# Mixture of experts in a five-layer block: rows gathered by expert through DRAM in 78 blocks of 128 rows, instead of all rows through each expert in use

## The reference, cut to what matters

```python
scores = sigmoid(xf @ gate_w + bias)
top_scores, top_idx = top_k(scores, 2)
top_scores = top_scores / (sum(top_scores) + 1e-06)
w = zeros((T, E)).at[arange(T)[:, None], top_idx].add(top_scores)
hact = gelu(einsum('th,ehi->tei', xf, up_w) + up_b)
eo = einsum('tei,eih->teh', hact, down_w) + down_b
combined = einsum('teh,te->th', eo * 0.1, w)
shared = (gelu(xf @ sw_up + sb_up) @ sw_down + sb_down) * 0.1
out = (shared + combined); out = out / (max(abs(out)) + 1e-06)
x = x + 0.5 * out
```

## Time and profile before

| | |
|---|---|
| median of 3 runs | 1553.57 us (1551.65 to 1554.36) |
| the profiled execution's own time | 1552.47 us |
| its span, first to last instruction | 1550.7 us |
| PE busy in the span | 1394.1 us (90%) |
| DVE, ACT, POOL busy | 61%, 52%, 26% |
| mean granted PE clock | 0.946 of full |
| m1 / m2 in the span | 664.1 to 965.5 / 1258.9 to the end |

### The profile page before, as it was taken

The page is one execution under the profiler, slowest core; times in us unless marked ns, Lnnn a source line. Parts: engine busy times, 40 slices in busy tenths (PEclk is TensorE's granted clock), DMA queues, the critical chain, the costliest instruction groups (busy, mean ns, idle before and its releaser), DMA issues. The chain is left out here.

```text
span 1550.7 us, 22874 instructions
## 1 busy us (share of the span) xinstructions
PE 1394.1 (90%) x7314; PEld 729.1 (47%) x7314; DVE 947.5 (61%) x1896; ACT 801.6 (52%) x1465; POOL 400.0 (26%) x585
## 2 busy tenths in 40 slices
PE   2896899999999879799999997899998779999997
PEld 1672222222222257567777764122221157777776
DVE  5677688889889347451222256699899941222236
ACT  0220688888888714354343354665666444443432
POOL 4021232322330012220000002788888710000000
PEclk9996799999999979889999998799999979999999
DMA  4020121222211010000000000444444300000001
GB/s 94 0 83 1 62 73 52 63 72 72 79 66 43 1 19 1 1 16 1 17 16 1 17 1 23 159 157 140 146 133 154 111 1 16 16 15 2 16 14 42
DMA packets 81206, 77.31 MB, mean 50 GB/s; under 512 B 21004, under 2 KB 60376, under 8 KB 81112
## 3 DMA queue, kind: packets, MB, share of 16 engines
q1 hardware_dynamic: 78992, 75.85, 15.7%
q10 hardware_dynamic: 2120, 0.28, 0.2%
HBM read 55.78 MB, written 16.78 MB: 47 GB/s over the span
## 5 line engine op out<-in xcount | busy, mean ns | idle before, releaser
L1375 ACT ACTIVATE m_hidden<-m_pU,m_up_b 128x512 f32<-128x512 f32 x320 | 219.8, 687 | 265.6 <-PE m_pU L1524 265.4
L1183 DVE TENSOR_REDUCE at_nm<-at_mx 128x2 f32<-128x1024 f32 x256 | 303.8, 1219 | 40.4 <-PE at_mx L1026 39.0
L1531 PEld LDWEIGHTS m_pD<-m_down,m_hidden 128*128 128x128 f32 x2560 | 296.7, 192 | 32.5 <-issue 32.5
L1531 PE MATMUL m_pD<-m_down,m_hidden 128*128 128x128 f32 x2560 | 297.1, 275 | 0.0
L1129 ACT ACTIVATE at_probs<-at_ring 128x512 f32<-128x512 f32 x512 | 269.2, 605 | 47.3 <-PE at_ring L1038 45.8
L1524 PE MATMUL m_pU<-m_xT_all,m_up 128*128 128x512 f32 x640 | 291.2, 601 | 1.1 <-PEq L305 0.5
L1500 DVE TENSOR_TENSOR m_out_b<-m_pD,m_down_b 128x512 f32<-128x512 f32 x64 | 44.2, 691 | 288.6 <-PE m_pD L1531 288.6
L1524 PEld LDWEIGHTS m_pU<-m_xT_all,m_up 128*128 128x128 f32 x640 | 118.0, 193 | 123.7 <-issue 123.5
L2023 POOL TENSOR_TENSOR ss_hc<-ss_h,ss_c_all 128x512 f32<-128x512 f32 x128 | 161.9, 1271 | 52.1 <-DVE ss_h L2195 44.6
L1038 PE MATMUL at_ring<-at_qq,at_kk 51*128 51x512 bf16 x512 | 163.3, 386 | 7.1 <-ACT at_probs L1129 6.1
L1026 PE MATMUL at_mx<-at_kk,at_qq 48*128 48x512 bf16 x512 | 156.0, 398 | 12.7 <-DVE at_nm L1183 8.1
(11 more groups left out here) (282 smaller groups left out, 1511.1 us busy)
## 6 DMA issues: line engine op xcount, KB each, us to landing
ss_dtb<-ss_dt_rows SPq DMA_DIRECT2D x128, 256.0 KB
at_qq<-q_stack SPq DMA_DIRECT2D x64, 96.0 KB, 2.3
at_kk<-k_stack SPq DMA_DIRECT2D x64, 96.0 KB, 2.3
q_stack<-at_qs SPq DMA_DIRECT2D x8, 384.0 KB, 2.6
k_stack<-at_ks SPq DMA_DIRECT2D x8, 384.0 KB, 3.0
ss_stack<-ss_parts SPq DMA_DIRECT2D x96, 32.0 KB, 2.7
X<-in_L_attn_x_dram SPq DMA_DIRECT2D x8, 256.0 KB, 6.1
q_stack<-at_qs SPq DMA_DIRECT2D x8, 256.0 KB, 2.9
```

What stands on the lines that cost most here:

```text
L1183: dve.tensor_reduce(nm[group % 2][:, 2 * (pair % 2) + parity, 2 * half:2 * half + 2], mx[parity][:, :, :], AX.X, ALU.max, negate=True).the ...
L1375: act.activation(hidden[t % 2][:, k, :], pU[k][:, :], ACT.Gelu, bias=up_b[buf][:, k:k + 1]).then_inc(s.gelu_done, 1)
L1531: last = pe.matmul(pD[t % 2][:, c, :], hidden[t % 2][:, k, c * P:(c + 1) * P], down[buf][:, k, :], start=(k == 0), stop=(k == NI - 1))
```

## The change

The dense passes of the listed experts are replaced by blocks of gathered rows; the shared expert's pass and the router stay.

- **Routing.** `hot[0]` and `hot[1]` stay apart, and `weight[k]` is each row's weight for its first and second expert. Two products on PE at t = 1 of the shared pass give each row's rank among the rows of its expert (`v.below`) and the totals. 16 links on DVE turn them into the row's place in a DRAM buffer, `index`, and into the expert of each block, `expert_of`. The chain of dependent steps has 37 links instead of 31.
- **Scatter.** The rows are cut into two halves of four sequences (`HALVES`). POOL scatters the rows of a tile of 128, with identity and weight behind them (130 floats, 520 bytes), to `sorted_rows` by an indirect transfer: 16 tiles for each half and choice, 64 transfers in all. Between the first and the second choice of a half it waits for the landing, since the same tile is marked anew.
- **Blocks.** Each expert's rows start on a multiple of 128 in the half's buffer, which has 39 blocks of 128 rows; all 2 x 39 = 78 are worked off whether they are full or not (8192 row-expert pairs fill 64). For block j SP loads the rows (`load_block`, ring of 8) and the expert's up weights (`load_up`, 256 KB, ring of 6); PE turns the rows (`turn`), ACT copies them, PE makes four up products with 128 columns, ACT four gelus of 128 x 128, PE four down products, DVE adds the bias and multiplies by the weight (ring `y` of 12), and POOL scatters the block to `pair_rows` (`put`), a second indirect transfer. All engines that need it read the block's expert by a register load. All experts' down weights stay in SBUF.
- **Return.** `pair_rows` is loaded for each sequence and choice (`load_results`) and added to `acc`, which now lies over `xT_all`. The first four sequences are finished in between the blocks of the second half, in five pieces each; the last four after the last block.
- **Scan's lead.** The same steps as before, spread over blocks of m1's second half (`LEAD_AT`, `LEAD_POOL_AT`, `SILU_AT`).
- **Elsewhere.** Both DRAM buffers are filled with an empty row from SP early in f1 (two transfers of 78 x 128 rows of 520 bytes), ahead of the first `write_stacks`; attention waits at its end for the fill. f2 and the scan write the normalised rows to a buffer for all rows (`v.rows`) and so wait for no transposition. A pair of barriers with a clearing of semaphores comes after m1. Biases of all experts are loaded in f2.

```diff
+HALVES = 2
+HS, HT = NB // HALVES, NT // HALVES
+HB = (2 * HT * P + E1 * (P - 1)) // P
+TB = HALVES * HB
+X_BUFS, Y_BUFS, T_BUFS, U_BUFS = 8, 12, 3, 6
+FINISH_AT, PIECES = 8, 5
+Y_LOAD_AT = {11: (0, 1), 18: (2,), 23: (3,)}
+LEAD_AT = {14: 3, 19: 4, 22: 5, 25: 6, 28: 7, 36: 8, 38: 9}
...
+def fill_sorted(sp, r):
+    sp.wait_ge(r.made, 2)
+    for rows in r.sorted:
+        sp.dma_start(rows.rearrange("(j p) d -> p j d", p=P), r.empty[:, :].unsqueeze(1).broadcast_to([P, TB, ROW])
+                     ).then_inc(r.filled, 16)
...
+            def load_block(j):
+                if j >= X_BUFS:
+                    sp.wait_ge(s.y_ready, j - X_BUFS + 1)
+                sp.dma_start(xb[:, j % X_BUFS, :], sorted_rows[j * P:(j + 1) * P, :]).then_inc(xb_in[j % X_BUFS], 16)
+            def load_up(j):
+                e = expert_at(sp, j)
+                if j >= U_BUFS:
+                    sp.wait_ge(s.bup_done, j - U_BUFS + 1)
+                sp.dma_start(up_now[j % U_BUFS][:, :], ins["L1_ffn_up_w"][e]).then_inc(up_in[j % U_BUFS], 16)
...
+            for half in range(HALVES):
+                for k in range(2):
+                    sp.wait_ge(scattered[half][k], 16 * HT)
+                for j in range(HB):
+                    load_block(half * HB + j)
+                    load_up(half * HB + j)
...
+            wait_written(TB)
+            for b in range(HS, NB):
+                load_results(b)
...
+            def scatter(half, k, t):
+                at_tile = half * HT + t
+                pool.indirect_dma_start(sorted_rows, bass.IndirectOffsetOnAxis(ap=index[:, k, at_tile:at_tile + 1], axis=0),
+                                        v.rows[:, at_tile, :], None, bounds_check=TB * P - 1, oob_is_err=False
+                                        ).then_inc(scattered[half][k], 16)
+            def put(j):
+                pool.wait_ge(s.y_ready, j + 1)
+                pool.indirect_dma_start(pair_rows, bass.IndirectOffsetOnAxis(ap=y_id[j % Y_BUFS][:, :], axis=0),
+                                        y[j % Y_BUFS][:, :], None, bounds_check=PAIR_ROWS - 1, oob_is_err=False
+                                        ).then_inc(y_out[j % Y_BUFS], 16)
...
+            pool.wait_ge(s.placed, 1)
+            for t in range(HT):
+                scatter(0, 0, t)
+            pool.wait_ge(scattered[0][0], 16 * HT)
+            mark(0, 1)
+            for t in range(HT):
+                scatter(0, 1, t)
+            mark(1, 0)
+            for t in range(HT):
+                scatter(1, 0, t)
+            pool.wait_ge(scattered[1][0], 16 * HT)
+            mark(1, 1)
+            for j in range(HB):
+                if j < HT:
+                    scatter(1, 1, j)
+                put(j)
...
+            for j in range(TB):
+                after = expert_at(act, j + 1) if j + 1 < TB else None
+                gelus(j, e)
+                if j + 2 < TB:
+                    take_turned(j + 2)
+                if lead is not None and j - HB in LEAD_AT:
+                    scan_lead_act(act, g, q=ahead, s=lead, t=LEAD_AT[j - HB])
...
+                if j >= Y_BUFS:
+                    dve.wait_ge(y_out[j % Y_BUFS], 16 * (j // Y_BUFS))
+                dve.wait_ge(xb_in[j % X_BUFS], 16 * (j // X_BUFS + 1))
+                dve.tensor_copy(y_id[j % Y_BUFS][:, :], xb[:, j % X_BUFS, ID:ID + 1])
+                dve.wait_ge(s.bdown_done, j + 1)
+                dve.tensor_tensor(yt[j % 2][:, :], pD[j % 2][:, 0, :],
+                                  v.down_b[:, bass.ds(e, 1), :].rearrange("p a d -> p (a d)"), ALU.add
+                                  ).then_inc(s.y_taken, 1)
+                dve.wait_ge(s.y_taken, j + 1)
+                dve.tensor_scalar(y[j % Y_BUFS][:, :], yt[j % 2][:, :], xb[:, j % X_BUFS, WEIGHT:ROW], None, ALU.mult
+                                  ).then_inc(s.y_ready, 1)
...
+            turn(0)
+            turn(1)
+            block_up(0)
+            for j in range(TB):
+                if j + 2 < TB:
+                    turn(j + 2)
+                if lead is not None and j - HB in LEAD_AT:
+                    scan_lead_pe(pe, g, q=ahead, s=lead, t=LEAD_AT[j - HB])
+                if j + 1 < TB:
+                    block_up(j + 1)
+                after = expert_at(pe, j + 1) if j + 1 < TB else None
+                block_down(j, e)
```

More of the change, by code:

```diff
@@ L153, in scale_rows @@
     for c in range(NC):
-        last = act.activation(out[:, c, :], g.X[:, b, c, :], ACT.Identity, bias=t.shift[:, b, c:c + 1],
+        last = act.activation(out[:, c, 0:D], g.X[:, b, c, :], ACT.Identity, bias=t.shift[:, b, c:c + 1],
                               scale=g.rstd[:, b, c:c + 1])
@@ L296, in _, with adapter_ffn @@
             dve.wait_ge(st, half + 1)
-def adapter_ffn(nc, g, w, sem, tag, rows=None, lead=None, ins=None, ahead=None):
+def adapter_ffn(nc, g, w, sem, tag, rows=None, lead=None, ins=None, ahead=None, experts=None, places=None):
     s = record(**{n: sem(f"{tag}_{n}") for n in (
@@ L342, in adapter_ffn @@
         behind = rows if rows is not None else lead
-        rows_xn = sb("rows_xn", [P, NC, D]) if rows is not None else None
         def has_next(b, ahead):
@@ L368, in _ @@
             take_rstd(pool, g, s.var, s.rstd, ones)
+            if lead is not None:
+                make_empty_row(pool, places)
             if rows is not None:
+                make_moe_constants(pool, experts)
                 for b in range(NB):
@@ L389, in transpose_rows @@
                 for c in range(NC):
-                    last = pe.transpose(pR[:, c, :], rows_xn[:, c, :], g.identf[:, :])
+                    last = pe.transpose(pR[:, c, :], experts.rows[:, b * NC + c, 0:D], g.identf[:, :])
                 last.then_inc(r.xT_done, 1)
@@ L1224, with dispatch_rows @@
 COMBINE = 0.1
+HALVES = 2
+HS, HT = NB // HALVES, NT // HALVES
+ROW = D + 2
+ID, WEIGHT = D, D + 1
+PAIR_ROWS = 2 * NB * L
+HB = (2 * HT * P + E1 * (P - 1)) // P
[4 more added lines that the diff above has]
+LEAD_AT = {14: 3, 19: 4, 22: 5, 25: 6, 28: 7, 36: 8, 38: 9}
+SILU_AT = 23
+SHIFT_AT = {12: 0, 17: 1}
+LEAD_POOL_AT = {30: (0, 1), 31: (2,), 32: (3,), 33: (4, 5), 37: (6, 7), 38: (8,)}
+def dispatch_rows(nc, sb, sem):
+    return record(
+        empty=sb("empty_row", [P, ROW]), filled=sem("rows_filled"), made=sem("empty_made"),
+        sorted=[nc.dram_tensor(f"sorted_rows{i}", (TB * P, ROW), F32, kind="Internal").ap() for i in range(2)],
+        pairs=[nc.dram_tensor(f"pair_rows{i}", (PAIR_ROWS, D), F32, kind="Internal").ap() for i in range(2)])
@@ new lines, in moe_weights @@
+def moe_weights(sb, sem):
+    return record(
+        up_b=sb("mw_up_b", [P, E1, NI]),
+        down_b=sb("mw_down_b", [P, E1, D]), rows=sb("mw_rows", [P, NT, ROW]),
+        ramp=sb("mw_ramp", [P, E1]), below=sb("mw_below", [P, P]), in_half=sb("mw_in_half", [P, HALVES * E1, HT]),
+        in_list=sb("mw_in_list", [P, HALVES, E1]), steps=sb("mw_steps", [P, HT]), blocks=sb("mw_blocks", [1, HB]),
+        base=sb("mw_base", [P, HALVES, E1]), ids=sb("mw_ids", [P, NT]), idw=sb("mw_idw", [P, 2, NT, 2]),
+        loaded=sem("mw_in"), made=sem("mw_made"))
@@ L1486, in finish @@
                     last.then_inc(s.x_done, 1)
-                    if out is None:
-                        last = take_stats(dve, g, b, s.x_done, b + 1)
+                if piece == 4 and out is None:
+                    last = take_stats(dve, g, b, s.x_done, b + 1)
                     if lead is not None and b < 2:
@@ new lines, in _ @@
+            dve.wait_ge(v.loaded, BIAS_LOADS)
+            e = expert_at(dve, 0)
+            for j in range(TB):
+                after = expert_at(dve, j + 1) if j + 1 < TB else None
+                if j >= Y_BUFS:
[9 more added lines that the diff above has]
+                                  ).then_inc(s.y_ready, 1)
+                e = after
+                jj = j - HB - FINISH_AT
+                if 0 <= jj < HS * PIECES:
+                    finish(jj // PIECES, jj % PIECES)
+                if lead is not None and j - HB == SILU_AT:
+                    silu(dve, lead, 0)
@@ L1893, in scan_lead_act, with selective_scan @@
             front(act, q, s, 1, n)
-        for n in (5, 7):
-            back(act, s, 0, n)
-def selective_scan(nc, g, q, lead, m2, ins, sem, tag):
+    if t in (8, 9):
+        back(act, s, 0, 5 if t == 8 else 7)
+def selective_scan(nc, g, q, lead, m2, v, ins, sem, tag):
     s, r = lead, m2.s
@@ L2135, in row_norm @@
                     act.wait_ge(r.shifted, lot_of(b) + 1)
-                    if b > 0:
-                        act.wait_ge(r.xT_done, b)
                 for c in (2 * half, 2 * half + 1):
-                    last = act.activation(rows[:, c, :], g.X[:, b, c, :], ACT.Identity, bias=row_shift[:, b, c:c + 1],
+                    last = act.activation(v.rows[:, b * NC + c, 0:D], g.X[:, b, c, :], ACT.Identity, bias=row_shift[:, b, c:c + 1],
                                           scale=g.rstd[:, b, c:c + 1])
```

(2 more changed lines are left out.)

607 lines of the change are left out of this document (345 added, 262 removed).

## The result

The changed kernel takes 1493.95 us (median of 4 runs, 1488.69 to 1496.05) against 1553.43 (4 runs, 1551.65 to 1554.36): a ratio of 0.9613, 95% interval 0.9587 to 0.964, so 59.5 us less. The forecast was 1485, 68 us less. The profiled execution has a span of 1490.9 us, 59.8 less than before.

What follows compares the result with a forecast made beforehand. PE's work in the two mixtures was taken as the bound. m1 28.8 us less and m2 40.0 less took the profiled 1552.5 to 1483.7; with the median 1.1 above, 1485 us, range 1455 to 1595.

Steps and rivals of the forecast that it cites:

- The lever and the pace: Both mixtures: PE's work bounds; a block takes 2.05 us (1.95 to 2.2), 78 blocks 160 us plus 1.5 for first gelus.
- The start: Each mixture's start: `index` ready at 17 us, 32 calls, first half in DRAM at 60.5, first up product at 64.
- X: Length of one indirect call on POOL: taken at 1.2 us, bounds 0.37 and 4.80.
- The y ring: First half's blocks: DVE needs `y` of block j - 12 written; at j = 27, 121 against PE's 123: just holds.
- The lead charge: m1's blocks: 18 us for the scan's lead on ACT and PE, one more table load included, bounds 11 and 22.
- The tails: Behind PE's last block: 27.7 us in m1 (9.5 before), 26.3 in m2 (11.6 before); barriers behind m1 1.4 more.
- POOL as the bound: Rival, both mixtures: POOL's calls decide from X = 1.74 on; 1629 us at X = 2.0; chance 0.14 beyond 1.74.
- The prediction's threshold: Both mixtures: from X = 1.74 on POOL decides; m1 299 and m2 297 us there, as before in sum.
- Its point at X = 1.5: First halves: PE stalls behind `y` by about 12 us and starts 10 later, 1520 us; in-between case's chance 0.14.
- The port: Rival, blocks: DVE's two SBUF operations wait for POOL's running call, 39 us a mixture, 1562 us; chance 0.08.
- Lost pace: Rival, blocks: hand-overs, transfers or lower clock make a block 2.5 us, 35 us a mixture, 1555 us; chance 0.10.
- The DMA term: Blocks: 384 packets at 49 ns on 16 engines, 1.2 us of each block's 2.05, bounds half that or 2.0.

Runs made afterwards that it cites:

- The ring of 20: The changed kernel with 20 places instead of 12 in the ring of block results `y`: 1486.74 us, ratio 0.9574.
- the second profile: The changed kernel itself, unchanged, profiled again in a later group on another chip: 1490.29 us, ratio 0.9586.
- the later lead: The changed kernel with the scan's first five lead pieces one or two blocks later in m1: 1598.69 us on a slow chip, 1488.99 (0.9577) on another.
- the first experiment: The changed kernel with m1's results loaded ahead of the scan's stack stores, POOL's lead pieces 6 and 7 after the last scatter: 1487.12 us, ratio 0.9589.

## Why the prediction was right, and where its terms were off

**The lever and the pace held.** PE's work was what counted, the blocks replaced four passes, and all that was costed at nothing stayed hidden: PE's register loads, the fill (PE's first use of the stacks starts at 136.4 where it was 135.6, and m1 as early as before), the transfers. A block takes 1.89 us. I had 2.05, with 1.95 as the lower bound, because I kept 0.13 us for hand-overs that lie beside the products; the bound was too high. (With the ring's stalls and the start, m2's mean is 1.96.) For 78 blocks and the first gelus that is 154.6 against 161.5 us in m2, 6.9 in the kernel's favour.

**The start: mis-sized, 69.7 and 68.9 us against 64.** In m1 the first call comes at 18.8 instead of 17: `index` is ready at 17.8, and the call follows 1.0 us later. The 32 calls and what stands between them take 44.3 us against 41.1. X was taken at 1.2 from the small power and is 1.275, of which 0.30 is not the call but the gap in front of it: 2.4 us over 32 calls. Five of the calls are longer, four of them beside DVE's additions: 1.6 us. The landing took 0.9 less. From SP's first issue to the first up product it is 5.1 us against 3.6, because that product stands behind the second block's turn, and that block's rows are issued 1.8 us after the first's. PE's pause of 8.7 us behind the shared pass is POOL's, as forecast. The shared pass itself ends at 60.9, not at 56.1; before, m2's took 59.5 (1258.90 to 1318.39), so the 56.1 was too short, and it changes nothing while PE waits for POOL.

**The y ring: it did not "just hold".** DVE waited for it 14 times in each mixture, from 2.55 us of POOL for two calls against 1.89 of PE, 0.66 a block where the forecast had 0.35 (2.4 against 2.05). The ring of 20 prices it at 3.5 us of PE's first half in m1 and 4.0 in m2, of which m2's second half gives 1.8 back.

**The lead charge: the largest miss, 24.2 us against 18** (178.8 - 154.6), outside my bounds of 11 to 22. In the second profile it is 28.4, with the same waits and a granted clock of 0.95 instead of 0.98 in m1's second half. 11.8 is PE's own work, and 12.8 are PE's five waits for ACT. I had ACT's bursts with their table loads, and not that ACT would stand in front of two pieces until their shift is made: 5.3 us. The expectations of the later lead put this down to POOL being behind with its scatters; the trace shows POOL within 1.1 us of DVE there, and DVE's statistics with POOL's 2.0 us for the shift as what comes late. Moving the pieces takes that away all the same and gives part of it back at piece 8.

**The tails.** m2's was 25.7 us against 26.3. m1's from PE's last product to the scan is 33.0 against 27.7 + 1.4: the finishes took their 19.3, the barriers 1.65, and the excess of 4.4 is the order on SP, which the first experiment removes. I read that order in the diff and did not cost it.

**The sum.** m1 is 8.8 us longer than forecast (+5.7 start, -0.7 for pace and lead together, +3.9 end), m2 2.7 shorter, and the scan 3.3 longer where I had nothing.

**The rivals.** POOL as the bound: X is 1.275, and POOL did not decide. The prediction's threshold is not what it says: by its own formulas POOL's 24.5 + 142X passes PE's 187.1 + 32X from X = 1.48 on in m2 and, with the lead, 1.64 in m1, and 1.74 is where the time equals that of the kernel before. Its point at X = 1.5, 12 and 10 us in each of two mixtures, adds up to 1529 and not 1520. The port: this rival's mechanism is there, at a fraction of its price. In the blocks DVE's operation from SBUF to SBUF has a median of 0.287 us; 15 of 156, all begun 0.46 to 0.65 us into a call, took 0.38 to 0.56, where the rival wanted a wait of 1.2 us each. At m1's end, beside POOL's own 1.3 us operations of the lead, four took 0.91 to 2.06. And in the other direction the eight calls shown above are 0.22 to 0.47 us longer than 0.97. For these calls the trace agrees with the waiting that the Trainium skill states ("SBUF — State Buffer", section "SBUF: two separate sides"). The figure of the Trainium skill for POOL's path ("DMA: Bandwidth & Descriptors", section "Specifications"), a time to the first byte, had given an estimate of X = 1.0 and 1472 us; the measured 1.275 decides. Lost pace: not in hand-overs. The DMA term was low, 1.2 us a block against 0.82 x 1.89 = 1.55 (results and output included), inside its bounds of 0.6 and 2.0; it is the thinnest cover in the kernel.

## What to carry to other kernels

An indirect call is here paid by the call, not by its rows: count calls per step of the bound engine and look at the gap in front of each, not at the busy time alone. Where an in-order engine would stand in front of somebody else's input, follow that input back to the step that really ends last before you name a cause, and place the taker behind it. Put what the next stage needs last behind what this stage waits for. Compare stages with the spread that unchanged stages have between profiles. Time a kernel that leans on such calls on more than one chip before it is taken for faster.
